# Attention probabilities turned in 32x32 blocks on VectorE and moved between partitions by DMA, in a graph transformer block on one core

## The reference, cut to what matters

```python
nx = ln(x, ln1_g, ln1_b)                     # x: (128, 128, 256)
q, k, v = heads(nx @ wq + bq), heads(nx @ wk + bk), heads(nx @ wv + bv)
bias = where(adj > 0, 0.1 * adj * adj, -inf)[:, None]
attn = softmax(q @ k.T / sqrt(32) + bias)    # (128, 8, 128, 128)
out = merge(attn @ v)
x1 = x + (out @ wo + bo)
n2 = ln(x1, ln2_g, ln2_b)
return x1 + gelu(n2 @ w1 + b1) @ w2 + b2     # w1: (256, 1024)
```

## Time and profile before

| | |
|---|---|
| median of 3 runs | 1563.25 us (1560.99 to 1565.13) |
| profiled execution | 1563.58 us, span of its core 1561.6 us |
| granted TensorE clock, mean | 0.985 |
| TensorE matmul busy | 1499.5 us, 96% of the span |
| ScalarE busy | 1156.5 us, 74% |
| VectorE busy | 1121.1 us, 72% |
| GpSimd busy | 546.4 us, 35% |
| packets of the DMA queue of SP | 55056, 45.38 MB, 9.3% of the 16 DMA engines |

### The profile page before, as it was taken

How to read it: one execution, slowest core, us unless ns; L and a number is a source line. 1 busy time by engine, 2 the same in 40 slices (tenths; PEclk the granted TensorE clock), 3 DMA queues, 4 the chain that set the end, 5 groups by cost and what they waited for, 6 DMA issues and landing times.

```text
span 1561.6 us, 35739 instructions
## 1 busy us (share of the span) xinstructions
PE 1499.5 (96%) x12604; PEld 1276.2 (82%) x12604; DVE 1121.1 (72%) x2130; ACT 1156.5 (74%) x3336; POOL 546.4 (35%) x392
## 2 busy tenths in 40 slices
PE   7789999999999999999999999999999999999988
PEld 6668888888888888888888888888888888888867
DVE  4677777767777777767777777777777767767653
ACT  3687778777778777768777778777778777778762
POOL 3334343324343323433324343324343323444100
PEclk8799999999999999999999999999999999999999
DMA  3001110011110011110011110011111011110000
GB/s 128 21 21 35 35 34 25 11 33 35 34 34 30 6 32 34 34 32 20 18 34 34 34 33 27 10 34 34 34 34 30 9 31 35 34 34 11 8 12 27
DMA packets 55124, 46.37 MB, mean 30 GB/s; under 512 B 3345, under 2 KB 54801, under 8 KB 55057
## 3 DMA queue, kind: packets, MB, share of 16 engines
q1 hardware_dynamic: 55056, 45.38, 9.3%
HBM read 28.58 MB, written 16.78 MB: 29 GB/s over the span
## 4 chain that ended last, share of the span: by engine, by line
PE 70%; ACT 12%; DVE 11%; issue 6%; DVEq 0%; DMA 0%; POOL 0%; ACTq 0%; SPq 0%; POOLq 0%
PE work L328 17%; PE work L329 15%; PE work L330 15%; PE turned L405 6%; ACT soft L611 6%; PE area L421 5%; DVE soft L780 4%; PE area L387 3%; PE area L328 3%; DVE nmax L784 3%; ACT hid L667 2%; DVE xt_lo L876 2%; ACT hid_parts L674 2%; PE turned L454 2%; PE area L330 2%
## 5 line engine op out<-in xcount | busy, mean ns | idle before, releaser
L611 ACT ACTIVATE soft<-soft,nmax 128x128 f32<-128x128 f32 x1024 | 396.9, 392 | 85.9 <-DVE nmax L784 85.6
L884 DVE TENSOR_TENSOR hid_parts<-hid,hid_parts 128x512 fp32r<-128x512 f32 x256 | 217.9, 851 | 182.9 <-ACT hid_parts L674 182.8
L967 POOL TENSOR_TENSOR ve<-mv,eps 128x4 f32<-128x4 f32 x64 | 13.0, 203 | 818.2 <-DVE mv L827 413.1
L328 PE MATMUL work<-w_hi,hid_parts 128*128 128x256 f32 x1024 | 295.6, 289 | 1.4 <-DVE res L895 1.0
L330 PE MATMUL work<-w_hi,hid_parts 128*128 128x256 f32 x1024 | 286.7, 280 | 0.0
L329 PE MATMUL work<-w_lo,hid_parts 128*128 128x256 f32 x1024 | 286.6, 280 | 0.0
L780 DVE TENSOR_TENSOR soft<-area,ebias 128x1024 f32<-128x1024 f32 x128 | 156.0, 1219 | 145.4 <-PE area L387 145.4
L667 ACT ACTIVATE hid<-work,b_col 128x512 f32<-128x512 f32 x256 | 176.0, 688 | 66.8 <-PE work L330 64.3
L328 PE MATMUL work<-nt_hi,w_hi 128*128 128x512 f32 x512 | 210.1, 410 | 1.7 <-DVE nt_lo L876 1.7
L652 ACT ACTIVATE qk_all<-work,bqk_col 128x512 f32<-128x512 f32 x128 | 87.0, 679 | 161.0 <-PE work L330 161.0
L329 PE MATMUL work<-nt_lo,w_hi 128*128 128x512 f32 x512 | 200.4, 391 | 0.0
(11 more groups left out here) (91 smaller groups left out, 3217.5 us busy)
## 6 DMA issues: line engine op xcount, KB each, us to landing
xin<-in_x SPq DMA_DIRECT2D x32, 512.0 KB, 4.0
out<-res SPq DMA_DIRECT2D x128, 128.0 KB, 1.7
adj_in<-in_adj SPq DMA_DIRECT2D x32, 256.0 KB, 4.2
w_raw<-in_L_gnn_w SPq DMA_DIRECT2D x1, 1024.0 KB, 9.4
soft<-in_L_gnn_w SPq DMA_DIRECT2D x1, 1024.0 KB, 11.6
wa_raw<-in_L_gnn_wq SPq DMA_DIRECT2D x1, 256.0 KB, 4.0
wa_raw<-in_L_gnn_wk SPq DMA_DIRECT2D x1, 256.0 KB, 6.6
wa_raw<-in_L_gnn_wv SPq DMA_DIRECT2D x1, 256.0 KB, 6.8
```

What stands on the lines that cost most here:

```text
L328: pe.matmul(o, lhs_hi, rhs_hi, start=first, stop=False)
L611: a = act.activation(soft[:, b % 2, h, :], soft[:, b % 2, h, :], ACT.Exp, bias=nmax[:, b % 2, h:h + 1], accum_out=rsum[:, b % 2, h:h + 1])
L884: dve.tensor_tensor(hid_lo[:, m, :], hid[:, m % 3, :], hid_hi[:, m, :].bitcast(F32), ALU.subtract).then_inc(hid_lo_ready, 1)
```

## The change

`turn` and `turned_copy` go, and with them the two banks of `turned`. In their place, for each graph:

- `turn_blocks` on VectorE: one transpose instruction over 128 partitions x 1024 elements, which turns each 32x32 block of `soft` by itself and writes `blocks` (memory of the weights' raw copy, `wa_raw`), sorted by block column.
- `shuffle` on SP: 16 DMAs, one for each pair of 32-row bands, from SBUF to SBUF, each 32 partitions x 1 KB, from `blocks` into `probt`, which now has two buffers.
- `mix` waits for the landing of the 16 (`landed`).

The division by the sum stays on VectorE, ahead of the transpose. `work` has four banks: three (0 to 2) are a ring for the flips, `v`, `qk`, `up` and `down`, given out by the fourth number of each entry of `UNITS`, and bank 3 holds `mixed` and `wout`. All engines have other orders, and the stages lie elsewhere: `up` 0 and 1 of group n-1 stand at the end of step n, `up` 2 to 7 in the next step; `stats2` and `norm2` of a group stand in the step after its scores. The exponential of a graph is two halves of 4 heads. The raw weights of the MLP are loaded into `res` and into the memory of `nhat` and `hid`.

```diff
-UNITS = ([("down", 0, -2), ("down", 1, -2), ("down", 2, -2), ("qk", 0, 1), ("down", 3, -2), ("qk", 1, 1),
+UNITS = [("proj", 0, -1, 3), ("up", 2, -2, 0), ("up", 3, -2, 1), ("mix", 1, -1, 3), ("up", 4, -2, 2),
...
-        mixed, wout = area[:, 0, D:2 * D], area[:, 2, D:2 * D]
-        turned = ps("turned", [P, 2, 512])
-        work = ps("work", [P, BANKS, 512])
+        work = ps("work", [P, 4, 512])
+        mixed, wout = work[:, 3, 0:D], work[:, 3, D:2 * D]
...
+            def shuffle(step, off, b):
+                if not step.has(off):
+                    return
+                sp.wait_ge(blocks_ready, step.through(off, GB, b))
+                for i in range(RPB):
+                    for j in range(RPB):
+                        sp.dma_start(probt[j * HD:(j + 1) * HD, b % 2, i, :, :],
+                                     blocks[i * HD:(i + 1) * HD, b % 2, j, :, :]).then_inc(landed[b % 2], 16)
...
             def body(step):
-                store(step, 0)
-                store(step, 1)
-                if step.has(0):
-                    load(step, 2, True)
-                store(step, 2)
-                store(step, 3)
+                shuffle(step, -1, 2)
+                load_adj(step, 2)
+                shuffle(step, -1, 3)
+                store(step, -2, 0)
+                shuffle(step, 0, 0)
+                store(step, -2, 1)
+                shuffle(step, 0, 1)
+                store(step, -2, 2)
+                load_x(step, 2)
+                store(step, -2, 3)
...
+            def turn_blocks(step, off, b):
+                if not step.has(off):
+                    return
+
+                if step.at_first(off) and b == 0:
+                    dve.wait_ge(bo_added, 1)
+                need(dve, full["mix"], step.through(off, GB, b - 2))
+                dve.wait_ge(normed, step.through(off, GB, b))
+                dve.transpose(blocks[:, b % 2, :, :, :],
+                              soft[:, b % 2, :, :].rearrange("p h (j k) -> p j h k", j=RPB))\
+                   .then_inc(blocks_ready, 1)
...
             def body(step):
-                edges_wait(step)
-                residual_start(step)
-                edges(step)
-                result_start(step)
-                rstd(step, 2, x_stats, mv1, ve1, x_veps, rstd1, x_rstd)
-                rstd(step, 0, n_stats, mv2, ve2, n_veps, rstd2, n_rstd)
+                rstd_of_n(step, -1)
+                result_start(step, -1)
+                residual_start(step, 0)
+                rstd_of_x(step, 2)
+                edges(step, 1)
```

More of the change, by code:

```diff
@@ L36 @@
 RPB = P // HD
+BLK = H * HD
 TOK = GB * P
@@ L490, in up @@
+            def up(step, off, m):
+                if not step.has(off):
                     return
@@ L638, in flip_hi @@
                 dst = xt_hi if kind == "xt" else nt_hi
-                for c in range(DC):
-                    act.wait_ge(full[kind], step.count(off, DC, c))
-                    act.activation(dst[:, c, :], turned[:, c, :], ACT.Copy)\
-                       .then_inc(hi_taken[kind], 1)
-            def query_key_copy(step, m):
-                if not step.has(1):
+                if c == 0 and kind == "xt":
+                    need(act, full["qk"], step.through(off - 1, 4, 3))
+                    need(act, full["v"], step.through(off - 1, 2, 1))
@@ L647, in query_key_copy @@
+                if c == 0 and kind == "nt":
+                    need(act, full["up"], step.through(off - 1, FC, FC - 1))
+                act.wait_ge(full[kind], step.through(off, DC, c))
+                act.activation(dst[:, c, :], work[:, bank_of(kind, c), :], ACT.Copy)\
+                   .then_inc(hi_taken[kind], 1)
+            def query_key_copy(step, off, m):
+                if not step.has(off):
                     return
-                act.wait_ge(full["qk"], step.count(1, 4, m))
@@ L668, in gelu, with hidden_hi @@
                                bias=b1_col[:, m:m + 1]).then_inc(taken["up"], 1)
-            def hidden_hi(step, m):
-                if not step.has(-1):
+            def hidden_hi(step, off, m):
+                if not step.has(off):
                     return
-                act.wait_ge(taken["up"], step.count(-1, FC, m))
+                if m == 0:
+                    need(act, full["down"], step.through(off - 1, GB, GB - 1))
+                act.wait_ge(taken["up"], step.through(off, FC, m))
@@ L825, in stats2 @@
+            def stats2(step, off):
+                if not step.has(off):
+                    return
+                dve.wait_ge(n_stat1, step.through(off, GB, GB - 1))
                 dve.memset(gate[:, :], 0.0)
@@ L930, in body @@
-                hidden_lo(step, 4)
-                residual(step, 3)
-                hidden_lo(step, 5)
-                stats2(step)
-                hidden_lo(step, 6)
-                hidden_lo(step, 7)
-                if not step.steady and step.n == -1:
-                    for k in range(4):
-                        late_lo(k)
-                    late_biases()
-                    late_rows()
+                norm1(step, 1, 0)
+                norm1(step, 1, 1)
+                residual(step, -1, 0)
@@ L942, in _ @@
+                turn_blocks(step, 0, 2)
+                if not step.steady and step.n == 0:
+                    late_lo()
             dve.wait_ge(cols_loaded, 16)
```

831 lines of the change are left out of this document (418 added, 413 removed).

## The result

The changed kernel takes 2081.97 us (median of 4 runs, 2080.73 to 2085.79), the kernel before 1562.12 us (4 runs, 1557.72 to 1565.13): a ratio of 1.3335, with a 95% interval from 1.3297 to 1.3373. I had forecast 1606 us. The direction holds, the size does not: the loss is 520 us, where I had 43, and my range ended at 1695. The profiled execution took 2080.73 us, its span 2078.9.

What follows compares the result with a forecast made beforehand. PE bounded the kernel before; after the change a chain through SP's shuffle and the load of x would, 47.3 plus 1.0 for the VectorE-POOL lock: 48.3 us a step. 252 + 28 x 48.3 gives 1604, plus 2: 1606 us, range 1512 to 1695.

Steps and rivals of the forecast that it cites:

- the fifth leg of the ring: On SP's queue: shuffle 5.8 us, a store 0.4, load of x 4.0 to landing, 0.1 waiting; from 37.0 to 47.3.
- the ring: Per step: statistics of x, PE and VectorE to the transpose of graph 1, SP's shuffle, next load of x; 47.3 us.
- What it adds: Added work per step: four block transposes of 1.2 us on VectorE, 64 small DMAs of 0.36 us on SP.
- Rival C: On SP, each small DMA costs 0.5 us, shuffle of graph 0 delays graph 1's: 51.9 a step, 1707 us; chance 0.18 with above.
- PE's 21.4 us of work: PE's leg from the projection of graph 0 to that of graph 3, in its new order: 21.4 us, ending at 24.7.
- the 1.0 of the lock: VectorE and POOL alternating on SBUF make PE late to graph 1's projection: between 0 and 2 us, taken as 1.0.
- a dear transpose: On VectorE, a block transpose of 2.6 us: two in series add 2.8, 50.1 a step, 1657 us; grouped with C, 0.18.
- start and end: Outside the 28 steps: first load of x at 58 us, 44 to the next, 150 after the last load.
- The legs in front of SP's: From the landing of x through VectorE, PE and POOL to the transpose of graph 1: 37.0 us, plus 1.0 for alternating.
- POOL's leg: Rival A: shuffles hardly load SP, POOL's `x1` decides: step 45.0 to 45.4, 1520 us; chance 0.19 including up to D.
- PE's bound: Rival B: the chain has slack and PE stays the bound, 42.5 to 43.4 a step, taken as 1470 us; chance 0.09.
- the sign: Whole kernel: a step of 46.8 us means no change; slower was given 0.65, same 0.07, faster 0.28.

## Why the prediction was wrong

**Wrong: the fifth leg of the ring, "SP: the shuffle 5.8".** It rests on the part "What it adds", where I took 0.36 us for each small DMA, with bounds of 0.3 and 0.5, from stores and loads. All of these have DRAM at one end. A DMA from SBUF to SBUF is another kind, and no row of before shows one: measured, 0.59 us of issue and 0.63 from start to start, outside of my bounds. The conclusion that the rows hardly matter was right; that the ends do not matter was taken for granted with it. A shuffle is 10.1 us, not 5.8.

**Wrong: the shuffles of graphs 2 and 3 were off the ring.** Rival C, the dear DMA, put only the shuffles of graphs 0 and 1 in series, and gave 51.9 us a step for 0.5. Its form with 0.63 gives 30.8 + 10.1 + 0.5 + 10.1 + 0.5 + 4.1 = 56.1, and 62.5 were measured. The missing 6.4 are in the first term, but for a load of x that lands 0.7 sooner and 0.4 of gaps: the shuffle of graph 0 began not 30.8 but 37.5 us after the landing of x (955.8 to 993.26), since the mix of graph 3 had to wait for two more shuffles of 10.0 each (the second item of the list by which the ring was added up). The prediction has no term for these two shuffles at any price: it takes them as covered by PE's 21.4 us of work. At 5 us each they are covered (eight of sixteen DMAs), at 10 they are not, and I did not ask at the price of C. PE's wait for `probt`, 278.4 us, is this. Rival C also leaves out the 1.0 of the lock, in its 51.9 as in the 50.1 for a dear transpose, while my own 48.3 contains it.

**Not foreseen: the clock.** I counted PE's legs at full clock. In the changed kernel PE waits 278.4 us for the shuffled probabilities and 220.0 for `attn_lo`, up to 9.4 and 12.2 at a time. After some of these waits (the 2.71 above) the granted clock stands at its lower level for a while, and PE is busy for 1534.0 us where I had 1360. Yet little of that lies on the ring, which holds only a mix and a `down` of PE: where the slow stretch meets them, the leg is 1.9 us longer, and the mean step of 63.07 is 0.6 above the common one of 62.5. If all of that is put down to the clock, it is worth some 17 us of the 520, by this estimate. No run changes the clock without changing the waits, so that this is read from the steps of one trace and not tried.

**Too small: start and end.** The first two loads of x lie at 67.41 and 128.91 us, 28 steps follow to the last at 1894.88, and 184.0 us follow that. I had 58 for the first, 44 for the step to the second, and 150 behind the last. That is 67.4, 61.5 and 184.0, 61 us more in all; with 28 x (63.07 - 48.3) = 414 from the steps it is 475, the whole difference between 1604 and the span of 2078.9. The short steps were not short: 61.5 us for the first, with four shuffles in it as in any other.

**Right.** The ring itself and its place, VectorE waiting for x before its statistics, though 14.3 us and not 4 to 6. The legs in front of SP's in their sum, 38.0 against 38.3 (one DMA for each shuffle); the 1.0 in it stands for a wait at the edge bias and not for the one that I had in mind. With eight DMAs the forecast ring, 5.1 in place of its 5.8, gives 47.6, and 47.8 was measured. The Trainium skill (SBUF — State Buffer, Who interferes with whom) has the lock, and the changed kernel's trace agrees: POOL's product `rstd`, 1.02 us in a free moment of that run, takes 1.89 at 927.15 us of the changed kernel. The block transpose, 1240 ns in 128 cases where I took 1.2:

```profile
L801 DVE STREAM_TRANSPOSE wa_raw<-soft 128x1024 f32<-128x1024 f32 x128 | 158.7, 1240 | 3.4
```

The prices of the alternatives: POOL's leg 45.0 (45.3 measured), PE's bound 42.5 to 43.4 (42.8 and 43.4). And the sign: a step above 46.8 loses, whatever PE gives back.

## What to carry to other kernels

Price a DMA by the pair of memories at its ends, and if the trace has no row of that pair, take a bound from outside of the rows at hand or measure it by itself. Multiply the issue time by the number of DMAs that a step puts in one queue: 64 at 0.63 us are 40 us of a step of 46.8, which, once the price is known, is visible before the kernel runs. Once a leg of a ring is stretched, follow again what was hidden beside it, at the dear price too; and when a data movement has to stay, few large DMAs through DRAM (five, in 4.0 us of queue) can beat many small direct ones (sixteen, in 10.1): here 1623 us against 2082, and 1469, less than the kernel before, once the load that the ring goes through is asked for earlier.

## What was not expected of the hardware

A DMA from SBUF to SBUF holds the issuing queue for 0.59 us in a series and 0.52 alone (one DMA for each shuffle), from DRAM to SBUF 0.42 (0.34 for the one that reads the shuffled blocks back), from SBUF to DRAM 0.33 to 0.37 for a store and 0.43 in the median of the series of four, on SP; from SBUF to SBUF it is about the same on ScalarE's queue (four in 2.72 us). That of a DMA from SBUF to SBUF does not depend on 16 to 128 rows nor on 256 bytes to 4 KB a row. The path through DRAM and back, with two landings in series, takes less than the issue of the direct one: the read begins 3.6 us after the first write (930.53 to 934.16) and lands 3.4 to 3.5 us later (the page's median), 7.1 in all, while the last of sixteen direct DMAs is issued 9.4 us after the first and lands 1.9 later, 11.3.
